# A transformer block on one core: expert gate and up weights loaded during attention, routed rows normalised on GpSimd

## What is computed

```python
x = x + xattn(layernorm(x), ctx_512, Wq, Wkv_expand, Wout)   # 16 heads, causal, 64 positions
x = x + bitlinear_mlp(layernorm(x), w_gate, g_gate, w_down, g_down)  # ternary weights, hidden 1024
x = x + moe(layernorm(x), gate_w, w_gate, w_up, w_down)

def moe(h, gate_w, w_gate, w_up, w_down):       # 16 experts of width 176, top 6
    scores = softmax(h @ gate_w.T)
    cw = top_k(scores, 6), zero elsewhere
    for e in range(16):
        y += cw[:, e] * ((silu(h @ w_gate[e].T) * (h @ w_up[e].T)) @ w_down[e].T)
```

## Time and profile before

| | us |
|---|---|
| median of three timed runs | 685.62 |
| lowest, highest | 684.96, 687.32 |
| the profiled execution | 684.45 |
| its span on the core | 682.9 |
| PE busy | 589.4 |
| DVE busy | 418.5 |
| ACT busy | 304.7 |
| POOL busy | 154.6 |

### The profile page before, as it was taken

How to read it: one execution, slowest core, us unless ns; L and a number is a source line. 1 busy time by engine, 2 the same in 40 slices (tenths; PEclk the granted TensorE clock), 3 DMA queues, 4 the chain that set the end, 5 groups by cost and what they waited for, 6 DMA issues and landing times.

```text
span 682.9 us, 10639 instructions
## 1 busy us (share of the span) xinstructions
PE 589.4 (86%) x3636; PEld 462.6 (68%) x3636; DVE 418.5 (61%) x784; ACT 304.7 (45%) x496; POOL 154.6 (23%) x207
## 2 busy tenths in 40 slices
PE   3789999856666657848999999999999999999995
PEld 2567777642334336637888888888888888888884
DVE  4737776759999966863545545544555454545543
ACT  3556566534999845632322232232232333322232
POOL 3627753027777726100000000000000000000000
PEclk9989999976999978987999999999999999999999
DMA  9400000001000008733222113222122212241211
GB/s 247 177 1 1 2 2 2 2 2 62 1 0 1 0 1 267 216 91 99 66 70 65 61 63 124 61 70 70 63 92 92 61 62 67 65 126 63 61 61 46
DMA packets 37353, 45.91 MB, mean 67 GB/s; under 512 B 10640, under 2 KB 24608, under 8 KB 37184
## 3 DMA queue, kind: packets, MB, share of 16 engines
q1 hardware_dynamic: 34224, 41.19, 20.0%
q0 software_dynamic: 1008, 3.67, 1.6%
q10 hardware_dynamic: 2080, 0.52, 0.4%
HBM read 41.04 MB, written 4.33 MB: 66 GB/s over the span
## 4 chain that ended last, share of the span: by engine, by line
PE 53%; DVE 1%; ACT 0%; issue 0%; DVEq 0%
PE psG L1420 6%; PE psY L1433 6%; PE psU L1420 6%; PE psG L1422 6%; PE psG L1421 6%; PE psU L1422 6%; PE psU L1421 6%; PE psY L1436 6%; PE psY L1435 6%; PE psT L1446 1%; DVE act_lo L1517 0%; DVE x_tok L1515 0%; DVE x_tok L1511 0%; DVE x_tok L1524 0%; ACT act_hi L1482 0%; ACT x_tok L1488 0%
## 5 line engine op out<-in xcount | busy, mean ns | idle before, releaser
L1482 ACT ACTIVATE act_hi<-x_tok 128x512 fp32r<-128x512 f32 x88 | 55.6, 632 | 197.1 <-DVE x_tok L1515 197.1
L1511 DVE TENSOR_TENSOR x_tok<-psU,x_tok 128x512 f32<-128x512 f32 x88 | 60.9, 692 | 110.1 <-PE psU L1422 110.1
L1517 DVE TENSOR_TENSOR act_lo<-x_tok,act_hi 128x512 fp32r<-128x512 f32 x88 | 61.0, 693 | 63.8 <-ACT act_hi L1482 63.8
L1476 ACT ACTIVATE x_tok<-psG 128x512 f32<-128x512 f32 x88 | 52.8, 600 | 49.4 <-PE psG L1422 49.4
L1420 PE MATMUL psG<-h3T_hi,wg_lo 128*128 (+1 forms) x176 | 69.8, 397 | 2.2 <-PEq L1121 2.2
L1433 PE MATMUL psY<-act_hi,wd_lo 128*128 128x512 f32 x176 | 68.9, 392 | 1.7 <-DVE act_lo L1517 1.6
L1422 PE MATMUL psG<-h3T_hi,wg_hi 128*128 (+1 forms) x176 | 69.0, 392 | 0.0
L1420 PE MATMUL psU<-h3T_hi,wu_lo 128*128 (+1 forms) x176 | 69.0, 392 | 0.0
L1421 PE MATMUL psG<-h3T_lo,wg_hi 128*128 (+1 forms) x176 | 69.0, 392 | 0.0
L1422 PE MATMUL psU<-h3T_hi,wu_hi 128*128 (+1 forms) x176 | 68.9, 392 | 0.0
L1421 PE MATMUL psU<-h3T_lo,wu_hi 128*128 (+1 forms) x176 | 68.9, 392 | 0.0
(11 more groups left out here) (220 smaller groups left out, 1162.4 us busy)
## 6 DMA issues: line engine op xcount, KB each, us to landing
cw_rows<-cw_spill SPq DMA_DIRECT2D x80, 128.0 KB, 2.9
cw_rows<-cw_spill SPq DMA_DIRECT2D x16, 224.0 KB, 2.9
cw_rows<-cw_spill SPq DMA_DIRECT2D x16, 192.0 KB, 2.8
w_stage<-in_L_ffn_w_gate_dram SPq DMA_DIRECT2D x11, 256.0 KB, 3.7
w_stage<-in_L_ffn_w_up_dram SPq DMA_DIRECT2D x11, 256.0 KB, 3.1
cw_rows<-cw_spill SPq DMA_DIRECT2D x16, 160.0 KB, 2.6
wg_nat<-in_L_attn_w_gate_dram SPq DMA_DIRECT2D x1, 2048.0 KB, 8.7
x_spill<-x_tok SPq DMA_DIRECT2D x1, 2048.0 KB, 7.6
```

The lines of the kernel that those rows point to most:

```text
L1476: nc.scalar.activation(a[s % 2][:, :], psG[s % 2][:, :], ACT.Silu).then_inc(s_silu, 1)
L1482: nc.scalar.activation(a_hi[s % 2][:, :], a[s % 2][:, :], ACT.Copy).then_inc(s_hi, 1)
L1511: nc.vector.tensor_tensor(a[s % 2][:, :], psU[s % 2][:, :], a[s % 2][:, :], ALU.mult).then_inc(s_t, 1)
L1517: nc.vector.tensor_tensor(a_lo[s % 2][:, :], a[s % 2][:, :], a_hi[s % 2][:, :].bitcast(F32), ALU.subtract).then_inc(s_lo, 1)
```

## The change

Two tensors are placed early: `raw`, 2 x 22 KiB per partition, takes all gate and all up rows in the order of memory. `wd_hi` and `wd_lo` are laid over its two halves. Unit 22, the first to write there, comes after unit 21, the last to read. SP issues `load_raw` twice in attention, behind `g_hid`, 2.75 MiB each. The ring `w_stage` now only carries down units; the first four of them (nine DMAs) are issued at the start of the bit-linear stage, the other seven (17 DMAs) in routing, by the old rule. PE waits for `raw_loaded` instead of the ring in units 0 to 21.

The odd tiles of a pair move from DVE to POOL. POOL forms the negated means of all tiles once (`less`) and then uses add, multiply for both tiles of a pair, under one semaphore `s_h`.

```diff
@@ attention_stage, sync
                 sp.dma_start(k.g_hid[:, :], g_down.unsqueeze(0).to_broadcast([P, INNER])).then_inc(k.bit_loaded, 16)
+                for m in range(2):
+                    load_raw(sp, k, m)
@@ bitlinear_stage, sync
-                for u in range(W_RING):
+                for u in range(RAW_UNITS, RAW_UNITS + W_RING):
                     load_unit(sp, k, u)
@@
+RAW_UNITS = 2 * (NCH // 2)
+def load_raw(eng, k, m):
+    rows = k.expert_w[m].rearrange("e f d -> (e f) d").rearrange("(c p) d -> p c d", p=P)
+    eng.dma_start(k.raw[:, m, :, :], rows).then_inc(k.raw_loaded[m], 16)
@@ route_stage, sync
-                for u in range(W_RING, units):
+                for u in range(RAW_UNITS + W_RING, units):
                     sp.wait_ge(s_wT, u - W_RING + 1)
                     load_unit(sp, k, u)
@@ route_stage, gpsimd
-                    n = 2 * i
-                    nc.gpsimd.tensor_scalar(h[:, i % 2, 0, :], k.x[:, n, :], k.mv[:, n, 0:1], rstd[:, n:n + 1],
-                                            ALU.subtract, ALU.mult).then_inc(s_h0, 1)
+                    for t in range(2):
+                        n = 2 * i + t
+                        nc.gpsimd.tensor_scalar(h[:, i % 2, t, :], k.x[:, n, :], less[:, n:n + 1], rstd[:, n:n + 1],
+                                                ALU.add, ALU.mult).then_inc(s_h, 1)
+                nc.gpsimd.tensor_scalar(less[:, :], k.mv[:, :, 0], -1.0, 0.0, ALU.mult, ALU.add).then_inc(s_less, 1)
@@ route_stage, vector
-                def row(i):
-                    if i > 1:
-                        dve.wait_ge(s_hT, i - 1)
-                    n = 2 * i + 1
-                    dve.wait_ge(s_rstd, 1 if i == 0 else 2)
-                    nc.vector.tensor_scalar(h[:, i % 2, 1, :], k.x[:, n, :], k.mv[:, n, 0:1], rstd[:, n:n + 1],
-                                            ALU.subtract, ALU.mult).then_inc(s_h1, 1)
-                row(0)
                 for i in range(NP + 1):
                     for n in range(UPT):
                         low(UPT * i + n)
-                        if n == 0 and i < NP - 1:
-                            row(i + 1)
@@ route_stage, tensor
-                    pe.wait_ge(k.w_loaded[u % W_RING], landed[u])
+                    if m < 2:
+                        pe.wait_ge(k.raw_loaded[m], 16)
+                    else:
+                        pe.wait_ge(k.w_loaded[u % W_RING], landed[u])
...
-                    pe.wait_ge(s_h0, i + 1)
-                    pe.wait_ge(s_h1, i + 1)
+                    pe.wait_ge(s_h, 2 * i + 2)
@@ build
+        raw_at = nc.sbuf_base
+        k.raw = b.sb("raw", [P, 2, NCH, D])
+        k.wd_hi, k.wd_lo = (nc.alloc_sbuf_tensor_at(f"wd_{p}", [P, NCH, D], F32R, offset=raw_at + n * NCH * D * 4)
+                            for n, p in enumerate(("hi", "lo")))
```

More of the change, by code:

```diff
@@ L1047 @@
 W_UNITS = [(m, j) for m in range(3) for j in range(NCH // 2)]
+RAW_UNITS = 2 * (NCH // 2)
 def unit_sources(k, u):
     m, j = W_UNITS[u]
+    assert m == 2
     first, end = 2 * P * j, 2 * P * (j + 1)
-    if m < 2:
-        rows = k.expert_w[m].rearrange("e f d -> (e f) d")[first:end, :]
-        return [(None, rows.rearrange("(c p) d -> p c d", p=P))]
     parts, col = [], first
@@ L1080, in route_stage @@
         rstd = b.sb("r_rstd", [P, NT])
+        less = b.sb("r_less", [P, NT])
         h = b.sb("r_h", [P, 2, 2, D])
@@ L1103, in route_stage @@
         units = len(W_UNITS)
-        (s_gwT, s_gwhi, s_gwlo, s_pool, s_rstd, s_h0, s_h1, s_hT, s_hi, s_lo) = (b.sem("r_" + n) for n in (
-            "gwT", "gwhi", "gwlo", "pool", "rstdd", "h0", "h1", "hT", "hi", "lo"))
+        (s_gwT, s_gwhi, s_gwlo, s_pool, s_rstd, s_h, s_less, s_hT, s_hi, s_lo) = (b.sem("r_" + n) for n in (
+            "gwT", "gwhi", "gwlo", "pool", "rstdd", "h", "less", "hT", "hi", "lo"))
         (s_lgT, s_lgTsb, s_lg, s_lgsb, s_ex, s_step, s_cw, s_cwT, s_wT, s_whi, s_wlo) = (b.sem("r_" + n) for n in (
@@ L1150, in _ @@
                     if part == 0:
-                        row(0)
+                        pool.wait_ge(s_less, 1)
+                        rows(0)
                 for i in range(1, NP):
-                    row(i)
+                    rows(i)
             @block.scalar
@@ L1268, in unit @@
                                 out, src = psW[u % 3][:, c, ch * P:(ch + 1) * P], \
-                                    k.w_stage[u % W_RING][:, ch, c * P:(c + 1) * P]
+                                    k.raw[:, m, 2 * j + ch, c * P:(c + 1) * P]
                             else:
@@ L1550, in build @@
         k.w_stage = [b.sb(f"w_stage{n}", [P, 2, 2 * P]) for n in range(W_RING)]
+        raw_at = nc.sbuf_base
+        k.raw = b.sb("raw", [P, 2, NCH, D])
+        k.wd_hi, k.wd_lo = (nc.alloc_sbuf_tensor_at(f"wd_{p}", [P, NCH, D], F32R, offset=raw_at + n * NCH * D * 4)
+                            for n, p in enumerate(("hi", "lo")))
+        k.raw_loaded = [b.sem(f"raw_loaded{m}") for m in range(2)]
         k.w_loaded = [b.sem(f"w_loaded{n}") for n in range(W_RING)]
@@ L1612, in build @@
             "wg_hi", "wg_lo", "wu_hi", "wu_lo"))
-        k.wd_hi, k.wd_lo = (b.sb(n, [P, NCH, D], F32R) for n in ("wd_hi", "wd_lo"))
         k.cw_stored = [b.sem(f"cw_stored{half}") for half in range(2)]
```

9 lines of the change are left out of this document (4 added, 5 removed).

## The result

The changed kernel is slower: 690.7 us in the median of 6 runs (690.08 to 691.64), against 686.04 of 6 runs of the kernel before beside it, a ratio of 1.0073 with a 95% interval of 1.0057 to 1.0089. The forecast was 684.9 with a range up to 687.3, so it missed on the slow side. The profiled execution took 690.64 us with a span of 689.1, 6.2 more than before.

What follows compares the result with a forecast made beforehand. PE bounds the kernel, mostly in the expert stage, which the diff was said not to touch; routing turns close through PE and ACT. An expert stage starting 0.7 earlier, other terms 0, gave 685.6 - 0.7 = 684.9 us, range 682.8 to 687.3.

Steps and rivals of the forecast that it cites:

- a cost in a place where the diff does nothing: Closing caveat: instruction supply or the clock in attention, while two loads fill the DMA engines behind g_hid; no size given.
- Gate and up loads leave routing: Routing: PE no longer waits for unit 4's load, a gain of 0.28 us.
- Start of the stage: Start of routing: POOL makes both tiles of a pair at 0.55 us each; pair 1 starts when it did, cost 0.
- The rival with 1.24 us a tile: Start of routing: POOL's tiles keep the old form's price, +2.0 us, 687.6; chance 0.07.
- Turns: Routing turns 2 to 7: PE and ACT set 3.39 us each, so taking an operation off DVE gains 0.
- The end: End of routing: down-weight loads start earlier, so unit 26 starts 0.66 us earlier and the expert stage with it.
- Attention: Attention: raw loads queued behind g_hid do not delay its landing, cost 0, upper bound 1 us.
- the prediction's own sign (ACT starting after 27): Attention: ACT's Abs pass was expected at 25.9; a start after 27 would prove a step wrong.
- The large rival (3 to 8 us): Attention: g_hid shares the DMA engines with the raw loads and lands 3 to 8 us late, 690; chance 0.07.
- The clock: Clock's return in routing and the expert stage: PE's pattern before both stays, so 0.
- the 0.9 of that rival: Expert stage: its clock returns sooner, -0.9 us more, 684.0; chance 0.14.
- Slower by more: Whole kernel: slower by over 0.3%, from g_hid's late landing and half of the slow POOL tiles' case; chance 0.12.

Runs made afterwards that it cites:

- place_only: The kernel before with only the down weights' two tensors allocated where the changed kernel has them: 690.23 us, 1.0064 of before.
- raw_top: The changed kernel with raw placed high, at 168960, so that h3T and all weights lie as in the kernel before: 684.98 us, 0.999 of before.
- after_raw64: The changed kernel with 64 bytes left free ahead of raw and 64 behind it: 684.95 us, 0.999 of before.
- rows_only: The kernel before with all row tiles on POOL in the add, multiply form, loads left in routing: 685.94 us, 0.9998 of before.
- late_raw: The changed kernel with SP waiting for all bit-linear loads, g_hid the last, before issuing the two raw loads: 690.48 us, 1.0065 of before.
- after_all128: The changed kernel with 64 bytes free ahead of h3T, so h3T, gate, up and activations start at multiples of 128 bytes: 685.66 us, 1.0003 of before.

## Why the prediction was wrong

**The step that failed** is the first sentence on what bounds the kernel: the expert stage holds most of the time, "The diff does not touch its products, so a gain must come from before it." The products' text is untouched, but their operands moved. The slower issue there cost 5.4 us (4.4 with what the earlier clock gave back) of the 6.2 us of the span, in the one stage that I had put aside. The sum had no term for it and no rival stood for it. The last sentence of the prediction did name "a cost in a place where the diff does nothing", but looked for it in attention. place_only, raw_top and after_raw64 show the cause, as far as the starts of the tensors.

**Gate and up loads leave routing, -0.28.** Right in kind, and over the 20 profiles somewhat small: no wait before unit 4 (it starts 0.12 us behind the last logits product, at 267.25), and unit 22 starts 28.6 us after the stage's start instead of 28.8. In the six kernels with raw it is 28.3 to 28.6, in the fourteen without 28.8 to 30.2, with the clock's phases in that spread.

**Start of the stage, 0.** Right: POOL's tile takes 548 to 559 ns in all 16 (two in 1.09 us above); pair 1 starts 6.8 us after the stage's start, against 6.9. The rival with 1.24 us a tile fell. The warning weighed there is for operations with two inputs; both forms of the tile read one tensor and two columns of scalars, so it bore on neither.

**Turns, 0.** Right: still 3.39 us (pairs at 269.51 and 272.90), and rows_only, where only DVE's share was taken off, is at 0.9998.

**The end, -0.66.** The term was too small for the mechanism: unit 26 starts 1.3 us earlier counted from the stage's start, not 0.66, and waits 0.20 instead of 0.76. From unit 22 on the forecast had three links: 0.68 us until SP issues, 2 x 0.51 for the pieces, 2.75 from the last issue to PE. The trace has 288.34 - 287.71 = 0.63, 2 x 0.504 (8.57 us for 17 pieces), and 291.47 - 289.35 = 2.12. The last is the mis-sized one, by 0.63; I had taken the middle of nine such links; why this one is shorter than all of them was not tried. By cw only 0.4 of the 1.3 us is left in this profile. The granted clock, at 0.5 from 297 us on, is the likely taker: in raw_top, whose clock was at 1.00 until 302 us, unit 26 starts 32.4 us after the stage's start, as here, and cw 44.5 instead of 45.3.

**Attention, 0 with a bound of 1.** Inside the bound, but not 0: with the raw loads directly behind it g_hid lands 10.4 to 10.6 us after its issue in five profiles, without them 9.5 to 9.9 in fourteen, and in late_raw, with the same loads behind a wait, 9.7. ACT's wait goes the same way. By the prediction's own sign (ACT starting after 27) the step was wrong in two of these kernels, after_raw64 and after_all128 at 27.71 and 27.15. My argument, that a later transfer does not pass an earlier one, is no argument that it does not slow it. I take 0.8 us from the middles of the two groups (10.5 and 9.7). By the Trainium skill, DMA: Bandwidth & Descriptors, section Latency and other measured facts, the estimate was up to 1.8 us; the traces have 0.8, so within it. The large rival (3 to 8 us) fell.

**The clock, 0.** The experts' clock came back after 3.2 us instead of 5.6 and gave the 0.9 of that rival; but in an execution whose clock had dropped before the end of routing. Whether the one belongs to the other was not tried, and neither is an effect of the change that one profile can show.

**The chances.** Slower by more is 0.07 and half of 0.07, 0.105, where 0.12 stands; nothing hangs on it.

**The sum, -0.7.** raw_top (0.999, 0.997 to 1.001) and after_raw64 (0.999, 0.9976 to 1.0005) are the change without the misplacement; -0.7 of 685.6 is 0.999. So far as it came out, it was by two errors that cancel: attention cost 0.8 where 0 was forecast, and routing gave 1.6 (by the middles above) where 0.7 was. The two kernels do not separate -0.7 from 0, so this is agreement and in part luck, not proof. after_raw64 is the best form of the changed kernel found, and not measurably faster than the kernel before.

## What to carry to other kernels

A change that allocates, frees or overlays a buffer touches every product whose operands lie behind it; print the starts of all tensors before and after, and look at them before putting any stage aside. Here a stage in which PE never waits took 1.5% longer (0.4% in one kernel) when a product's weights and its moving operand started on different kinds of 64-byte multiples, and 64 bytes of padding gave it back; a matmul's issue step (227 or 231 to 236 ns), not its wait, is where such a loss shows. When two profiles differ where the diff has nothing, run the allocation alone first.

## What the runs showed of the hardware that I had not expected

- The step from one 128x512 fp32r matmul to the next at a granted clock of 1.00 is 226.5 to 227.0 ns with weights and moving operand on the same kind of start (but for those issued behind slow ones), and on average 229.1 to 233.1 ns for products on different kinds; in seven of eight kernels the 6 or 12 products behind them run at 230.0 to 231.5 though their own operands are alike. A whole group costs 0.3 to 1.6 us more on 90.8.
- This does not follow VectorE's work, and it repeats: 92.14 and 92.14 us for the two groups of the changed kernel read above.
- POOL normalises a 128x256 fp32 tile in 0.55 us with add and multiply, where subtract and multiply had taken 1.24. The mean then came from x_mv and now from a tensor of its own, so the operation alone is not shown to be the cause.
